# Scaled attention outputs and query rows turned by DMA transposes instead of TensorE, and the jobs dealt anew

## The reference, cut to what matters

```python
q = rms_norm((x @ wq).reshape(B, L, 16, 128), q_norm_w)          # 16 heads, 4 key heads
k = rms_norm((x @ wk).reshape(B, L, 4, 128), k_norm_w)
k_ctx = rms_norm((h_ctx_kv @ wk_ctx).reshape(B, T, 4, 128), k_norm_w)
q, k = q * cos + rotate_half(q) * sin, k * cos + rotate_half(k) * sin
k_full, v_full = concat([k_ctx, k]), concat([v_ctx, v])
...
probs = softmax(einsum('bhqd,bhkd->bhqk', q, k_full) * scale + causal_mask)
out = einsum('bhqk,bhkd->bqhd', probs, v_full).reshape(B, L, 2048) @ wo
```

## Time and profile before

| | |
|---|---|
| median of 3 runs | 1299.98 us (1299.79 to 1300.78) |
| profiled execution, its own time | 1299.34 us |
| its span, first to last instruction | 1297.5 us |
| PE, DVE, ACT, POOL busy | 92%, 78%, 64%, 61% of the span |
| mean granted TensorE clock | 0.976 of full |

### The profile page before, as it was taken

One profiled execution on the slowest core, in us unless ns is written; L12 is line 12 of the kernel. 1 busy time (PEld: TensorE's weight loads), 2 busy tenths in 40 slices (PEclk: granted clock), 3 DMA queues, 4 the chain that ended last, 5 costly groups with the idle time before them and its releaser, 6 DMA issues.

```text
span 1297.5 us, 30487 instructions
## 1 busy us (share of the span) xinstructions
PE 1193.7 (92%) x11547; PEld 893.8 (69%) x11547; DVE 1015.4 (78%) x1979; ACT 832.3 (64%) x1917; POOL 790.8 (61%) x1010
## 2 busy tenths in 40 slices
PE   4998699999999999999999999999999976777898
PEld 2544477877787777778777777777777765455557
DVE  6876768888688888788888878888888887776673
ACT  4755567776677676767677677777777644446431
POOL 2765386867668585857668595857768533761000
PEclk9998999999999999999999999999999998789999
DMA  8620067576867687695767677676778898000000
GB/s 286 201 82 15 18 137 163 129 159 134 187 135 154 143 148 149 128 209 130 159 132 152 145 148 147 133 160 139 151 145 153 161 193 222 1 1 1 1 1 33
DMA packets 507298, 164.94 MB, mean 127 GB/s; under 512 B 485488, under 2 KB 500352, under 8 KB 506896
## 3 DMA queue, kind: packets, MB, share of 16 engines
q1 hardware_dynamic: 506128, 159.57, 56.5%
q0 software_dynamic: 1024, 3.42, 1.0%
HBM read 33.05 MB, written 8.26 MB: 32 GB/s over the span
## 4 chain that ended last, share of the span: by engine, by line
PE 69%; DVE 16%; DMA 5%; POOL 3%; ACT 3%; issue 3%; SPq 2%; POOLq 0%; DVEq 0%; ACTq 0%
PE PS L1217 14%; PE PS L1219 13%; PE PS L1218 13%; PE PS L1369 7%; PE PS L1365 7%; PE PS L1366 7%; DVE mx L1722 5%; DVE pl L1742 3%; DMA pT_l<-pl 2%; DMA pT_h<-ph 2%; PE PS L1318 1%; PE PS L706 1%; PE PS L684 1%; DMA sin<-in_c_sin 1%; DVE f_s L1653 1%
## 5 line engine op out<-in xcount | busy, mean ns | idle before, releaser
L1722 DVE TENSOR_REDUCE mx<-PS 128x1 f32<-128x512 f32 (+2 forms) x512 | 296.5, 622 | 123.8 <-PE PS L1219 122.6
L1365 PE MATMUL PS<-v_h,pT_h 128*128 128x129 f16 (+1 forms) x1856 | 225.8, 222 | 9.9 <-DMA pT_h<-ph 9.9
L1959 POOL CAST ph<-pr_end 128x705 f16<-128x705 f32 (+1 forms) x128 | 109.9, 858 | 200.4 <-ACT pr_end L1517 200.4
L1366 PE MATMUL PS<-v_l,pT_h 128*128 128x128 f16 (+1 forms) x1856 | 225.8, 221 | 0.0
L1365 PEld LDWEIGHTS PS<-v_h,pT_h 128*128 128x128 f16 (+1 forms) x1856 | 182.7, 98 | 14.0 <-DMA pT_h<-ph 11.3
L1217 PE MATMUL PS<-kT_h,qT_h 128*128 128x512 f16 (+2 forms) x512 | 181.9, 355 | 7.6 <-ACT pr L1517 7.6
L1517 ACT ACTIVATE pr<-PS,nb 128x1024 f32<-128x1024 f32 x128 | 144.0, 1125 | 68.9 <-DVE nb L1730 68.9
L1366 PEld LDWEIGHTS PS<-v_l,pT_h 128*128 128x128 f16 (+1 forms) x1856 | 183.0, 99 | 2.4
L1218 PE MATMUL PS<-kT_l,qT_h 128*128 128x512 f16 (+2 forms) x512 | 181.0, 354 | 0.0
L1219 PE MATMUL PS<-kT_h,qT_l 128*128 128x512 f16 (+2 forms) x512 | 180.8, 353 | 0.0
L1742 DVE TENSOR_TENSOR pl<-pr,ph 128x1024 f16<-128x1024 f32 x128 | 169.3, 1322 | 0.0
(11 more groups left out here) (287 smaller groups left out, 2964.4 us busy)
## 6 DMA issues: line engine op xcount, KB each, us to landing
stage<-in_ctxT SPq DMA_DIRECT2D x8, 800.5 KB, 6.6
weights_kept<-relay SPq DMA_DIRECT2D x30, 128.0 KB, 2.3
relay<-in_w_lanes SPq DMA_DIRECT2D x14, 204.9 KB, 3.6
stage<-in_wq SPq DMA_DIRECT2D x4, 512.0 KB, 4.0
stage<-in_wo SPq DMA_DIRECT2D x4, 512.0 KB, 3.8
pT_h<-ph SPq DMA_TRANSPOSE x128, 3.6
pT_l<-pl SPq DMA_TRANSPOSE x128, 3.6
ctx_kept<-ctx_h SPq DMA_DIRECT2D x2, 800.5 KB, 8.1
```

Of the source, the lines that this page charges most:

```text
L1365: mm(PS[:, OB, 0:DH + 1], pT_h[0:rows, slot, t, :], v_h[0:rows, par, v, :], start=t == 0, stop=False)
L1366: mm(PS[:, OB, 0:DH], pT_h[0:rows, slot, t, :], v_l[0:rows, par, v, :], start=False, stop=False)
L1722: dve.reduce_max(mx[:, c:c + 1], PS[:, c, 0:cols(u % LT, c)], AX_X).then_inc(mx_part, 1)
L1959: pool.tensor_copy(ph[:, slot, HALF:LAST + w], pr_end[:, 0:BANK + w]).then_inc(pool_hi, 1)
```

## The change

**Queries.** `kq` steps 0 and 6 are gone. In their place a job `("q", lt)` does no work on TensorE: ScalarE rounds the normed and rotated query rows in SBUF to `qn_h`, VectorE subtracts to `qn_l`, and SyncE turns both with two DMA transposes straight into `qT_h` and `qT_l` (`turn_queries`), for tile 0 behind the transposes of unit 4 and for tile 1 behind those of unit 5. There is one `qn_h` and one `qn_l` for both tiles, so ScalarE waits before it writes `qn_h` until the other tile's transposes have landed (`turned_q`).

**Outputs.** `o_scale` writes the high part of the scaled output as f16 (`o_n`, two buffers), a new VectorE instruction `out_low` makes the low part, and SyncE turns both with one DMA transpose (`turn_out`) between the two transposes of the unit after next. The jobs `("out", 0)` and `("out", 1)` are now the products by `wo`. TensorE's `pv` waits for `out_low` of the unit before (it waited for `o_scale`).

**Jobs, banks, reload.** `JOBS_AT` and `POOL_AT` are dealt anew; the banks go round over the whole run instead of starting with each group. `bring_back` reloads a slot in four transfers, behind units 0 to 3 of groups 3 and 7. In the last group the products by `wo` come later among the first steps of the tail.

```diff
-KQ_STEPS = 7
-JOBS_AT = [[("out", 0), ("out", 1), ("piece", 1)],
-           [("piece", 2), ("piece", 3), ("piece", 4)],
-           [("piece", 5), ("kq", 0), ("piece", 6)],
-           [("piece", 7), ("kq", 6), ("piece", 8), ("kq", 5)],
-           [("piece", 9), ("kq", 4), ("kq", 1)],
-           [("kq", 2), ("kq", 3)],
-           [("out", 2), ("out", 3)],
+KQ_STEPS = 5
+JOBS_AT = [[("piece", 1)],
+           [("out", 0), ("piece", 2), ("piece", 3)],
+           [("out", 1), ("piece", 4), ("q", 0), ("piece", 5)],
+           [("piece", 6), ("q", 1), ("piece", 7)],
+           [("piece", 8), ("kq", 5), ("piece", 9), ("kq", 4)],
+           [("kq", 1), ("kq", 2), ("kq", 3)],
+           [],
            [("piece", 0)]]
 JOB_LIST = [j for jobs in JOBS_AT for j in jobs]
-OUT_JOBS = [j for j in JOB_LIST if j[0] == "out"]
+RING = [j for j in JOB_LIST if j[0] != "q"]
...
-POOL_AT = [["q00", "q01"], [(1,), "q10"], ["q11", (2, 3)], ["k", (4, 5)], [(6, 7), (8, 9)], [], [], [(0,)]]
+POOL_AT = [["q00", "q01"], [(1,), "q10"], ["q11", (2, 3)], ["k", (4, 5)], [(6, 7)], [(8, 9)], [], [(0,)]]
...
+        qn_h = sm("qn_h", [P, BANK], F16)
+        qn_l = sm("qn_l", [P, BANK], F16)
...
-        o_s = sm("o_s", [P, LT, REP, DH], F32)
-        oT_h = sm("oT_h", [P, LT, BANK], F16)
-        oT_l = sm("oT_l", [P, LT, BANK], F16)
+        o_n = sm("o_n", [P, 2, 2, DH], F16)
+        oT = sm("oT", [P, LT, REP, 2, P], F16)
...
+                if n >= 2:
+                    turn_out(n - 2)
...
+            def turn_out(n):
+                lt, h = n % UNITS % LT, n % UNITS // LT
+                if n % UNITS < LT:
+                    wait(sp, oj_mm, (n // UNITS - 1) * LT + lt + 1)
+                sp.wait_ge(o_low, n + 1)
+                sp.dma_start_transpose(oT[:, lt, h, :, :], o_n[:, n % 2, :, :].rearrange("p k n -> p (k n)"))\
+                  .then_inc(turned_o[n % 2], 16)
+            def turn_queries(lt, g):
+                par = g % 2
+                sp.wait_ge(q_lo, g * LT + lt + 1)
+                for t, rows in ((qT_h, qn_h), (qT_l, qn_l)):
+                    sp.dma_start_transpose(t[:, par, lt * REP:(lt + 1) * REP, :], rows[:, :]).then_inc(turned_q[lt], 16)
             def group(g, last=False):
                 for u in range(UNITS):
                     turn(g, u)
+                    if u in (4, 5) and not last:
+                        turn_queries(u - 4, g + 1)
                     if u == 0 and 0 < g < NG - 1:
                         lane_load(g)
+                    if g in (KVH - 1, 2 * KVH - 1) and u < 2 * DC:
+                        bring_back(g // KVH, u)
...
-            def bring_back(slot, groups_done):
-                sp.wait_ge(pc_mm, NP * groups_done)
-                for k, t in enumerate((ctx_h, ctx_l)):
-                    sp.dma_start(t[:, slot, :, :].rearrange("p c n -> p (c n)"), kept[slot, k, :, :])\
-                      .then_inc(ctx_moved, 16)
+            def bring_back(slot, part):
+                if part == 0:
+                    sp.wait_ge(pc_mm, NP * KVH * (slot + 1))
+                t, c = (ctx_h, ctx_l)[part // DC], part % DC
+                sp.dma_start(t[:, slot, c, :], kept[slot, part // DC, :, c * SC:(c + 1) * SC]).then_inc(ctx_moved, 16)
...
-                    pe.wait_ge(ctx_moved, 64 + 64 * (g // (2 * KVH)))
+                    pe.wait_ge(ctx_moved, 64 * max(1, g // KVH))
...
-                    pe.wait_ge(rope_done, g * len(ROPES) + ROPES.index(f"q{lt}1") + 1)
-                    for j in range(REP):
-                        last = pe.transpose(PS[:, bank, j * P:(j + 1) * P], qr[:, lt * REP + j, :], ident[:, :])
...
-                if i < LT:
-                    pe.wait_ge(o_done, (g + 1) * UNITS - LT + i + 1)
-                    for h in range(REP):
-                        last = pe.transpose(PS[:, bank, h * P:(h + 1) * P], o_s[:, i, h, :], ident[:, :])
-                    last.then_inc(ot_tr, 1)
-                    return
-                lt = i - LT
-                pe.wait_ge(ot_lo, g * LT + lt + 1)
+                pe.wait_ge(turned_o[i], 16 * REP * (g + 1))
                 for h in range(REP):
-                    last = three(PS[:, bank, 0:D],
-                                 (oT_h[:, lt, h * P:(h + 1) * P], oT_l[:, lt, h * P:(h + 1) * P]),
+                    last = three(PS[:, bank, 0:D], (oT[:, i, h, 0, :], oT[:, i, h, 1, :]),
...
+                if u < LT and c == 0:
+                    pe.wait_ge(turned_q[u], 32 * (g + 1))
...
-                wait(pe, o_done, n)
+                wait(pe, o_low, n)
...
+            def q_hi_part(lt, g, par, bank=None):
+                n = g * LT + lt
+                act.wait_ge(rope_done, g * len(ROPES) + ROPES.index(f"q{lt}1") + 1)
+                wait(act, turned_q[1 - lt], 32 * ((n + 1) // 2))
+                copy(qn_h[:, :], query_rows(lt)).then_inc(q_hi, 1)
...
-                act.wait_ge(rd_done, unit_no(g, u) + 1)
-                copy(o_s[:, u % LT, u // LT, :], PS[:, OB, 0:DH], rden[:, u % 2:u % 2 + 1]).then_inc(o_done, 1)
-            def out_hi_part(i, g, bank):
-                if i < LT:
-                    wait(act, oj_mm, (g - 1) * LT + i + 1)
-                    act.wait_ge(ot_tr, g * 2 + i + 1)
-                    copy(oT_h[:, i, :], PS[:, bank, :]).then_inc(ot_hi, 1)
+                n = unit_no(g, u)
+                act.wait_ge(rd_done, n + 1)
+                wait(act, turned_o[n % 2], 16 * (n // 2))
+                copy(o_n[:, n % 2, 0, :], PS[:, OB, 0:DH], rden[:, u % 2:u % 2 + 1]).then_inc(o_done, 1)
...
+            def q_lo_part(lt, g, par, bank=None):
+                dve.wait_ge(q_hi, g * LT + lt + 1)
+                dve.tensor_tensor(qn_l[:, :], query_rows(lt), qn_h[:, :], ALU.subtract).then_inc(q_lo, 1)
...
+            def out_low(n):
+                dve.wait_ge(o_done, n + 1)
+                dve.scalar_tensor_tensor(o_n[:, n % 2, 1, :], PS[:, OB, 0:DH], rden[:, n % 2:n % 2 + 1], o_n[:, n % 2, 0, :],
+                                         ALU.mult, ALU.subtract).then_inc(o_low, 1)
...
+                before = unit_no(g, u) - 2
+                if not ahead and before >= 0:
+                    out_low(before)
                 if ahead:
                     for c in range(CHUNKS):
+                        if c == 2 and before >= 0:
+                            out_low(before)
```

More of the change, by code:

```diff
@@ L501, in build, with prep_user, job_bank @@
         PREP_BANKS = [TB, TB + 1, OB, XB]
+        prep_at = [sum(k != "q" for k, _ in PREP_JOBS[:n]) for n in range(len(PREP_JOBS))]
         def prep_bank(n):
-            return PREP_BANKS[n % len(PREP_BANKS)]
-        def job_bank(job):
-            return XBS[JOB_LIST.index(job) % len(XBS)]
+            return PREP_BANKS[prep_at[n] % len(PREP_BANKS)]
+        def prep_user(n):
+            if PREP_JOBS[n][0] == "q" or prep_at[n] < len(PREP_BANKS):
+                return None
+            return [j for j in PREP_JOBS if j[0] != "q"][prep_at[n] - len(PREP_BANKS)]
+        def job_bank(job, g):
+            if job[0] == "q":
+                return None
+            if g >= NG - 1:
+                return XBS[job[1]]
+            return XBS[(g * len(RING) + RING.index(job)) % len(XBS)]
         def target(job, g):
@@ L812, in tail_pe, with tail @@
                         "up1": up_second, "ht1": turn_experts, "dn1": down_second}
-            def tail():
-                for key, hf, i in TAIL_PE[TAIL_FRONT["pe"]:]:
+            def tail(start, end=None):
+                for key, hf, i in TAIL_PE[TAIL_FRONT["pe"]:][start:end]:
                     if key[:2] == "tr":
@@ L1110, in tail_dve, with tail @@
                         "mu": experts, "hl1": lambda hf, j: hidden_lo(hf, j, "hx1", "hl1"), "az": add_second}
-            def tail():
-                for key, hf, i in TAIL_DVE[TAIL_FRONT["dve"]:]:
+            def tail(start, end=None):
+                for key, hf, i in TAIL_DVE[TAIL_FRONT["dve"]:][start:end]:
                     if key[:2] == "st":
@@ L1435, in _ @@
             turn_first(0, 1)
-            for i, before in ((1, (("out", 3), NG - 2)), (2, (("out", 0), NG - 1)), (3, (("out", 1), NG - 1))):
-                wait_bank(pe, *before)
-                out_proj(i, NG - 1, job_bank(("out", i)))
-            tail()
+            wait_bank(pe, ("out", 0), NG - 2)
+            out_proj(0, NG - 1, job_bank(("out", 0), NG))
+            tail(0, 2)
+            wait_bank(pe, ("out", 1), NG - 2)
+            out_proj(1, NG - 1, job_bank(("out", 1), NG))
+            tail(2)
         @block.scalar
@@ L1537, in weight_piece_hi @@
                 copy(piece_h, piece_f, WS).then_inc(pw_hi, 1)
-            kinds = {"out": out_hi_part, "piece": piece_out, "kq": kq_hi_part,
+            kinds = {"out": lambda i, g, bank: None, "piece": piece_out, "kq": kq_hi_part, "q": q_hi_part,
                      "mean": lambda i: None}
@@ L1592, in _ @@
             copy_first(0, 1)
-            out_hi_part(1, NG - 1, job_bank(("out", 1)))
             tail()
```

(10 more changed lines are left out.)

94 lines of the change are left out of this document (46 added, 48 removed).

## The result

The changed kernel takes 1460.86 us (median of 4 runs, 1460.41 to 1462.04) against 1300.38 for the kernel before in the same session (4 runs): 1.1227 times as long, 95% interval 1.1199 to 1.1254. The forecast was 1430 with a range of 1380 to 1475.

The account below looks back on a forecast made before the run. TensorE was taken to set the pace in the 15 groups that prepare a next one. Per group -1.8 + 6.4 + 1.2 + 2.8 = +8.6 us; 15 groups +129, reload +2, on 1299.3: 1430 us, range 1380 to 1475.

Parts of the forecast that it names:

- The mechanism: Iteration 3: tile 0's query transposes queue behind pT_l of unit 4, land at 722.2; ScalarE, then TensorE, wait for them.
- (b): Rival: DMA engines become a bound too, with slow issues and larger small waits; 13.3 us a group, 1509; chance 0.10 over 1475.
- ScalarE's wait: In job ("q", 1) of iteration 3, ScalarE waits for the other tile's query transposes to land: 8.8 us.
- TensorE's gap: TensorE stands still before chunk 0 of unit 6, waiting for unit 5's first exponential: 6.4 us once a group.
- The relief: TensorE loses two query and two output transpose blocks a group, 0.44 us each: 1.8 us a group saved.
- The clock: The granted clock falls behind TensorE's idle gap in each group: 1.2 us a group lost, ends 0 and 1.7.
- The smaller waits: TensorE waits for out_low (1.4), the moved norm (0.9), banks and low parts (0.5): 2.8 us a group, ends 0 and 4.5.
- The reload: Old idle times and slow clock go (-6.1); four-part transfers delay transposes, 4 us a reload: net +2, -6 to +10.
- The last two groups: Last group has no queries to prepare; its last output's DMA transpose is covered by the tail's first steps; nothing charged.
- (a): Rival: shorter wait, landing at 721.5, no clock loss; 4.4 us a group, about 1360; chance 0.10 for 1310 to 1385.
- (c): Rival: query transposes land before ScalarE needs them, only the relief and the reload's gain are left: 1267; chance 0.03.
- (d): Rival: the wait is hidden but the small waits eat the relief: +9, 1300 to 1310; chance 0.03.

Follow-up runs that it names:

- e1_two_q: Changed kernel with one buffer of query rows for each of the two tiles (qn_h and qn_l doubled): 1324.99 us, 1.0192 times the kernel before.
- e2_early: Changed kernel, single query buffer kept, tile 0's query transposes moved from behind unit 4 to behind unit 3: 1325.46 us, 1.0184 times the kernel before.
- e6_hybrid: Kernel before with queries by DMA, the reload in four parts, outputs on TensorE and a table with key steps moved: 1278.6 us, ratio 0.9823.
- e4_reload: Kernel before with only the four-part reload behind units 0 to 3 of groups 3 and 7: 1293.34 us, ratio 0.9935.
- e3_busy: Changed kernel with 28 unread 512-column matmuls in each group ahead of the scores of unit 6: 1433.64 us, 1.1011 times the kernel before.
- e9_norm_back: Changed kernel with two query buffers and GpSimd's norm of pieces 8 and 9 back in iteration 4: 1320.76 us, 1.0157 times the kernel before.
- e8_lowfirst: Changed kernel with two query buffers and out_low ahead of all four maxima on VectorE: 1317.23 us, 1.0131 times the kernel before.

## Why the forecast was right, and where its terms were off

**The mechanism holds, step by step.** The forecast counted 5.4 us from the end of VectorE's `p_lo` to the landing of the query transposes (716.8 to 722.2); measured are 5.35 (805.05 to 810.4). Three errors cancel in it. The forecast let 0.4 us of `out_low` pass between `p_lo` and the issue of `pT_l`, and nothing stands there (805.05, 805.08). The query issues take 1.28 and 1.26 us, not 0.5 each. And the second transpose lands 2.5 us after its issue starts, where 3.0 were taken. So that the landing came out to 0.05 us is luck; the chain of waits is not. The forecast's late end of the landing, 724.7, does not follow from its own terms as written, either: with an issue of 1.4 us the second transpose starts at 720.1 and lands by 723.7, which makes the longest gap 7.9 and not 8.9 us, and rival (b) 1 us a group cheaper. From landing to the end of the exponential 2.8 us were forecast and 2.8 passed. ScalarE's wait: 8.8 forecast (8.7, as the copy in the earlier trace rows ends at 713.53), 9.18 seen. TensorE's gap: 6.4 forecast, 6.58 seen. e1_two_q and e2_early show by two independent edits that this wait, with the slow clock behind it, is the cause of 136 of the 161 us, and not only something that stands beside it.

**The relief** of 1.8 us a group is borne out only for the half of the queries. TensorE's busy time in a group falls from 57.29 to 56.40 in e6_hybrid: 0.89 for two blocks, as 2 x 0.44; only there does it show as time, 15 us against e4_reload. With the outputs' half as well it falls to 56.19 (e2_early), only 0.2 more, where the forecast has 0.9 more; why is not shown. No run turns the outputs alone. e2_early, with both halves, is 47 us slower than e6_hybrid, with the queries alone and another table, so in the form they have here the outputs and their table cost more than they relieve; which of the two costs it was not separated.

**The clock** is the term that was mis-sized: 1.2 us a group, bounds 0 to 1.7; e3_busy measured 2.3. The forecast scaled the loss behind the first reload. It counted one of the two stretches there, 1.3 us; with the other, 0.07 x 6, they lose 1.7. Here the clock falls inside the gap (1.00 up to 810, 0.62 as the mean of the next 4 us) and is still low when all the scores have run: at half the clock the two means put the slow stretch from 811.0 to 817.8, so 4.5 us of it lie behind the gap and lose 2.25. A bound from the rows would have been the slow clock over the whole of the next dense work: the scores took 2.26 us, and at half the clock they take that much more.

**The smaller waits** were put at 2.8 us; in the changed kernel they come to about 3.1 (25.2 for the norm, 23.8 for `out_low`, 5.6 for low parts, less 7.8 before, over 15 groups) and in e1_two_q to 3.3. The parts were less right than the sum: the norm costs 1.7 a group in the changed kernel instead of 0.9, the low parts nothing instead of 0.5 (in e1_two_q 0.7 more than before). And e9_norm_back shows that they may not be added as if each were lifted by itself.

**The sum.** In the windows of group 9 TensorE is busy for 58.53 us against 57.29 and idle for 9.57 against 0.61. That is 57.9 - 1.1 (relief) + 2.3 (clock) + 6.6 (gap) + 2.4 (what other idle time was added) = 68.1; the forecast had 57.9 - 1.8 + 6.4 + 1.2 + 2.8 = 66.5. The relief was taken 0.7 too large and the clock 1.1 too small; the small waits, 0.4 too large in this group, offset a part (the 3.1 above is the whole run's, with those ahead of group 0 and in the last groups). The difference of 1.7 us a group (68.2 against 66.5), 25 us in 15 groups, is most of the 31 that the forecast fell short by. The busy share in a group, forecast near 87%, is 58.53 of 68.10, or 86%.

**The reload** was priced at +2 (gain 6, delays 8). The delays hardly came: group 3 lasts 68.2 as any other and group 7 68.9. In the kernel before, groups 2 and 6 had lost 4.4 and 1.7 us. So this term was 7 us too high, and e4_reload gives its gain alone, 0.65%.

**The last two groups** were priced at nothing and cost 10 us: group 14 is 4.4 above its like (1.4 before), group 15 7.1 above the one before. SyncE in group 15 of the changed kernel, the windows of that stretch, and TensorE behind it:

```profile
1231.37 7.80 SPq L1187 DMA_TRANSPOSE pT_l<-pl  x1
```

```profile
1232.00:1236.00 4.00, 0.00 (x0) 0.00 (x0) 3.17 (x10) 0.79 (x1) 3.69 (x5) 0.77 1.06 110
1236.00:1240.00 4.00, 0.48 (x5) 0.48 (x6) 0.00 (x0) 2.18 (x4) 1.51 (x6) 0.50 1.35 117
```

```profile
1239.52 0.29 PE L1400 MATMUL PS<-v_h,pT_h 128*128 128x129 f16 x1 [8.42 <-DMA pT_h<-ph]
```

The DMA share is above 1.0 (1.06 and 1.35), the issue of one transpose takes 7.80 us, and TensorE idles 8.42 us for the `pT_h` behind it. Whether the outputs' transposes bring this about stays open. For it: the long issue of `pT_l` is in the changed kernel, e1_two_q, e3_busy, e8_lowfirst and e9_norm_back (5 to 8 us, group 15 at 55 to 59 us), and no `pT_l` takes that long in group 15 of the kernels with outputs on TensorE (50 to 51 us). Against it: e2_early has these transposes and its group 15 takes 50.3 us. No run isolates it; it may be a matter of which transfers meet there.

**The rivals.** (a), a shorter wait, fell with the gap of 6.58. (b), the DMA engines as the bound, is not what the middle shows (share 0.72; e1_two_q reaches 0.83), though one of its ingredients, issues of 1.3 us, is true. (c) and (d) needed the transposes to land before ScalarE wants the buffer; e1_two_q takes that need away and e2_early all but meets it, and the result is neither (c)'s 1267 nor (d)'s 1300 to 1310 but 1325, because the small waits and the last groups together outweigh relief and reload by 25 us. The Trainium skill, "VectorE: DVE Perf Modes", section "Rules for kernel authors", which the forecast weighed, asks only for the destination. e6_hybrid turns its queries by DMA and is the fastest kernel here, so the trace does not bear it out as a price. What counts is whether somebody waits for the landing.
